# First attention: who adds the relative terms in the two slots of eight that hold two maxima, PE instead of DVE

## What is computed

```python
dist = jnp.clip(jnp.arange(s)[:, None] - jnp.arange(s)[None, :], -MAX_REL, MAX_REL) + MAX_REL   # MAX_REL = 128
rel_pos = rel_emb[dist]
scores = jnp.einsum('bhqd,bhkd->bhqk', q, k)
scores = scores + jnp.einsum('bhqd,qkd->bhqk', q, rel_pos)
scores = scores / np.sqrt(HEAD_DIM).astype(np.float32)
attn = jax.nn.softmax(scores, axis=-1)
local_ctx = jnp.einsum('bhqk,bhkd->bhqd', attn, v)
```

## Time and profile before

| | before |
|---|---|
| median of 3 executions | 3952.41 us (3950.79 to 3961.33) |
| the profiled execution | 3964.92 us, span 3963.1 us |
| PE busy in the span | 3197.3 us (81%) |
| DVE busy | 2230.7 us (56%) |
| ACT busy | 2098.4 us (53%) |
| pair part of groups 0, 1, 2, 3 | 110.34, 111.20, 105.05, 111.19 us |
| all of the first attention's loop, about 127 to 740 us of the span | 613 us |

### The profile page before, as it was taken

One profiled execution on the slowest core, in us unless ns is written; L12 is line 12 of the kernel. 1 busy time (PEld: TensorE's weight loads), 2 busy tenths in 40 slices (PEclk: granted clock), 3 DMA queues, 4 the chain that ended last, 5 costly groups with the idle time before them and its releaser, 6 DMA issues. The chain is left out here.

```text
span 3963.1 us, 72945 instructions
## 1 busy us (share of the span) xinstructions
PE 3197.3 (81%) x24437; PEld 1667.2 (42%) x24437; DVE 2230.7 (56%) x3463; ACT 2098.4 (53%) x3805; POOL 1069.3 (27%) x967
## 2 busy tenths in 40 slices
PE   2788888518920899994699999999999999999997
PEld 1222323113310233331366556556556655655654
DVE  6767677572240777776455555555555555555553
ACT  1466566302210366663366666666666666666664
POOL 0000000003401111110454344345434534533541
PEclk6667587659965799997799999999999999999998
DMA  5221111204445011112211111111111111111111
GB/s 189 81 71 38 54 61 57 75 1 105 101 34 31 23 25 28 26 25 54 100 39 47 39 43 49 30 48 51 33 40 42 50 29 49 53 29 45 42 38 39
DMA packets 191921, 199.77 MB, mean 50 GB/s; under 512 B 113781, under 2 KB 120581, under 8 KB 186794
## 3 DMA queue, kind: packets, MB, share of 16 engines
q1 hardware_dynamic: 154218, 193.05, 17.7%
q10 hardware_dynamic: 37344, 1.97, 1.0%
HBM read 99.64 MB, written 28.97 MB: 32 GB/s over the span
## 5 line engine op out<-in xcount | busy, mean ns | idle before, releaser
L2383 POOL TENSOR_TENSOR tr_t<-tr_t 128x512 f32<-128x512 f32 x384 | 488.9, 1273 | 706.0 <-DVE tr_t L2227 706.0
L2390 POOL TENSOR_TENSOR tr_nq<-tr_t,tr_rn 128x512 f32<-128x512 f32 x384 | 392.6, 1044 | 395.0 <-ACT tr_rn L2123 387.6
L1595 DVE TENSOR_REDUCE attn_mp<-attn_ps 128x1 f32<-128x512 f32 (+3 forms) x660 | 395.2, 656 | 163.9 <-PE attn_ps L1446 86.5
L2088 ACT ACTIVATE tr_pr<-tr_ps 128x768 f32<-128x768 f32 x264 | 213.9, 810 | 375.3 <-PE tr_ps L1910 374.9
L2226 DVE TENSOR_TENSOR tr_t<-tr_ps,tr_tab 128x512 f32<-128x512 f32 x384 | 263.2, 685 | 243.2 <-ACT tr_sq L2097 243.1
L1925 PE MATMUL tr_ps<-tr_w,tr_xs 128*128 128x512 f32 x768 | 372.3, 607 | 29.7 <-DVE tr_xs L2254 26.2
L1557 ACT ACTIVATE attn_pr<-attn_ps 128x768 f32<-128x768 f32 (+2 forms) x352 | 300.9, 870 | 168.1 <-PE attn_ps L1479 165.2
L2236 DVE TENSOR_TENSOR tr_o<-tr_ps,tr_rd 128x384 f32<-128x384 f32 (+1 forms) x264 | 144.0, 545 | 429.3 <-ACT tr_rd L2113 414.0
L678 DVE TENSOR_REDUCE attn_mcol<-attn_ps 128x1 f32<-128x1024 f32 x274 | 332.9, 1220 | 90.8 <-PE attn_ps L523 88.2
L663 ACT ACTIVATE attn_pr<-attn_ps 128x512 f32<-128x512 f32 x512 | 277.8, 599 | 160.6 <-DVE attn_ps L692 146.4
L1910 PE MATMUL tr_ps<-tr_qT,tr_kT 64*128 64x96 f32 (+1 forms) x4224 | 300.9, 282 | 0.0
(11 more groups left out here) (259 smaller groups left out, 5037.2 us busy)
## 6 DMA issues: line engine op xcount, KB each, us to landing
tr_v<-tr_va SPq DMA_DIRECT2D x144, 192.0 KB, 2.6
attn_ka<-scratch_kp SPq DMA_DIRECT2D x72, 294.0 KB
tr_v<-tr_va SPq DMA_DIRECT2D x144, 128.0 KB, 2.4
moe_cb<-scratch_combineT SPq DMA_DIRECT2D x32, 512.0 KB
tr_w<-in_w_half SPq DMA_DIRECT2D x12, 1024.0 KB
tr_v<-tr_va SPq DMA_DIRECT2D x48, 256.0 KB, 2.4
scratch_kp<-proj_parts SPq DMA_DIRECT2D x36, 256.0 KB
attn_km<-scratch_kp SPq DMA_DIRECT2D x72, 98.0 KB
```

The source lines that it names most:

```text
L1595: dve.tensor_reduce(dst, src, AX.X, ALU.max).then_inc(maxed, 1)
L2383: pool.tensor_tensor(t12[:, slot, i, 0, :], t12[:, slot, i, 0, :], t12[:, slot, i, 1, :], ALU.add).then_inc(summed, 1)
L2390: pool.tensor_tensor(nq[:, slot, i, :].rearrange("p (h e) -> p h e", e=DH), t12[:, slot, i, 0, :].rearrange("p (h e) -> p h e", e=DH), rn[ ...
```

## The change

In slots 3 and 7 (`PE_ADDS`) DVE no longer adds. PE does it: behind the bf16 score matmuls of a unit it multiplies `rel` (moving, fp32, 256 or 128 columns) with the fp32 identity (stationary, 128 x 128) and accumulates into the same columns of the bank. ACT's exponential then waits for PE's count (`qk_done`) and no longer for DVE's. In all slots the matmul on the near tiles now comes last of its unit.

```diff
+PE_ADDS = tuple(J for J in range(ST) if TILES_J[J] > 1)
...
 def adds_until(a):
-    return sum(1 for x in range(a + 1) if near_tiles(x // 4, x % 2))
+    return sum(1 for x in range(a + 1) if x // 4 not in PE_ADDS and near_tiles(x // 4, x % 2))
...
-                for v, lo, hi in ((1, 0, near[0]), (0, *near), (2, near[1], S)):
+                for v, lo, hi in ((1, 0, near[0]), (2, near[1], S), (0, *near)):
...
+                if J in PE_ADDS and near_tiles(J, c):
+                    first, count = near_tiles(J, c)
+                    D_ = first - J + 1
+                    mm = pe.matmul(ps[:, unit % 3, (first - 4 * c) * P:(first - 4 * c + count) * P], ident[:],
+                                   rel[:, 2 * p + e, J, D_:D_ + count, :].rearrange("p d i -> p (d i)"), start=False,
+                                   stop=True, skip_group_check=True)
                 mm.then_inc(qk_done, 1)
...
-                            if near_tiles(J, c):
+                            if J not in PE_ADDS and near_tiles(J, c):
                                 act.wait_ge(rel_added, GP * ADDS * g + ADDS * p + adds_until(a) + 1)
...
-                if near is None:
+                if near is None or J in PE_ADDS:
                     return
```

## The result

| | before | after |
|---|---|---|
| median, runs side by side on one chip | 3956.85 us (3950.79 to 3961.33, 4 runs) | 4013.11 us (3992.00 to 4016.53, 4 runs) |
| ratio | 1 | 1.0137 [1.0110, 1.0164] |
| profiled execution, span | 3964.92, 3963.1 us | 4013.86, 4012.1 us |
| PE, DVE, ACT busy | 3197.3, 2230.7, 2098.4 us | 3258.7, 2203.4, 2100.4 us |

The account below looks back on a forecast made before the run. No engine was full; DVE was taken to end slot 3's waits. PE's charges in slots 3 (9.6 + 19.6) and slots 7 (3.5 + 2.9) made 35.6 us, on the median 3952.41 giving 3988 us; range 3956 to 4012 us.

Parts of the forecast that it names:

- Which engine ends the slot: Slot 3: DVE ends the waits before; with DVE off the chain PE is next, 4.7 us instead of 3.67 when fast.
- The price of the identity matmul: Slots 3 and 7: 0.48 us for 256 columns, 0.27 for 128; at the lower clock 0.91 and 0.49.
- the dense price: fp32 passes priced from dense rows with loads hidden: about 0.24 us for 256 columns, 0.136 for 128.
- the forecast's own sum: PE's new work less its idle time: slots 3 9.6 and 19.6, slots 7 3.5 and 2.9, together 35.6 us.
- the upper bound named for it: The fp32 weight load of 0.19 us stands bare before each of the 192 passes: 36 us more.
- DVE's relief is worth nothing: Slots 3 and 7: 37 us of DVE's adds removed, but PE then ends a fast slot 3, so no gain.
- The clock, taken as unchanged: Pair parts: granted clock unchanged on balance, for two opposite reasons; wrong if its mean leaves 0.78 by more than 0.05.
- The new place for a fall: Slot 4 starts behind a full PE and is light itself, so the clock may fall there; no size given.
- The near matmul last: All slots: writing the near matmul last of its unit costs nothing, since the unit is counted only at its end.
- The rest of the program as before: Everything after 780 us, outside the pair parts, stays as before.
- The 0.2 us: Each PE burst ends in some 0.2 us another matmul could use; four bursts in slot 3 free 0.8 us.
- rival 1: Slots 3 and 7: PE has more room, 0.8 us more free in slot 3; sum 18, 3970 us, chance 0.14.

Follow-up runs that it names:

- the kernel with slot 3 alone: The changed kernel with PE's adds in slot 3 only, DVE adding in slot 7 again: 4028.19 us, ratio 1.0158 to before.
- with 64 columns: The changed kernel with its fp32 identity matmuls cut to 64 columns each, the other near columns getting no relative term: ratio 1.0156 to before.
- The kernel without any adds: The changed kernel with the near tiles' relative terms in slots 3 and 7 added by neither DVE nor PE: 3964.10 us, ratio 1.0013.
- the kernel with the order alone: The changed kernel with all adds left to DVE, only the near matmul written last of its unit: 3952.14 us, ratio 0.9999.
- the changed kernel with dummies: The changed kernel plus two dummy bf16 matmuls ahead of the maximum tile in slots 0 and 1 of every pair: 3992.41 us, ratio 1.0102.

## Why the prediction was right

The sign and the place were right; one term was mis-sized.

- **Which engine ends the slot.** Right. Slots 3 and 7 are PE's from end to end; ACT's waits there are put down to PE, 69.5 us. The forecast for slot 3 was 4.7 and 7.9 us, measured 5.30 and 8.94; for slot 7 4.2, measured 4.53. I had called the mechanism wrong below 3.7.
- **The price of the identity matmul.** This is the step that failed: "I take the dense price, since those rows are of the same kind, with their loads hidden." Between these bf16 score matmuls the dense price didn't hold, whether it is the loads or the height. A matmul took 0.63 us of PE for 256 columns and 0.42 for 128 instead of 0.48 and 0.27, and 1.15 and 0.72 instead of 0.91 and 0.49 at the lower clock. Put into the forecast's own sum, which leaves its idle times as they are, these give 9 x 2.10 - 3.90 = 15.0, 7 x 3.74 = 26.2, 12 x 1.26 - 8.01 = 7.1, and 3 x 2.30 + 1.26 - 3.54 = 4.6 us: 53 instead of 35.6. With the slot lengths now measured, at the clock pattern of before, it reads: 9 fast threes x 1.63 = 14.7, 7 slow threes x (8.94 - 5.07) = 27.1, 12 sevens x 0.63 = 7.6, and about 4 for the last sevens (an estimate, since three of them stand at the lower clock in the earlier trace rows and none in the changed profile: a slow seven grew from 5.30 us in the kernel with slot 3 alone to 7.22, by 1.92, of which some 0.6 would fall into idle time as it did with 64 columns). Together about 53 again; measured were 48.5 between the two profiles, whose slots do not stand at the same clocks. The term was short by 13 to 18 us, and the upper bound named for it, 72 us with every load bare, about 20 too high.
- **DVE's relief is worth nothing.** Right, for more than the reason given. I had it that PE takes over. The kernel without any adds shows that the relief would be worth nothing even for free (slot 3 takes 3.67 us with DVE's adds and without any, and the ratio is 1.0013): the chain runs through the second tile and its maximum. The reading that DVE's adds end the waits of slot 3 was wrong in that. DVE's busy time fell by 31 us in the pair parts instead of 37.
- **The clock, taken as unchanged.** Its mean went from 0.79 to 0.80, within the 0.05 named. But that rests on a profile of before that stands 12.5 us above its median; against the 0.83 of the kernel with the order alone it fell, and cost 25 us. The runs show how much room the assumption had: the same slots gave 425 to 438 us between executions, and edits like this one gave clocks from 0.69 to 0.80. The new place for a fall that was named, slot 4 behind a full slot 3, is there in the changed kernel with dummies: in two pairs of group 3 the clock is 0.89 in slot 4 and 0.50 in slots 5 to 7.
- **The near matmul last: nothing.** Right, 0.9999.
- **The rest of the program as before.** Right here, within 3 us; with other edits in the same place the transformer moved by 16, which I had not thought of.
- **The range.** 3956 to 4012 us. The change brought 54 us instead of 36, and by the ratio 4006.6 lies in it, near its upper end; the bare median of these runs, 4013.11, lies 1.1 us above it, and the interval of the ratio, to 4017.2, reaches beyond it. That a sum short by a third still ended inside was in part luck.

The 0.2 us that I had estimated from the earlier trace rows at the end of each burst had spoken for rival 1, with more room on PE than charged. The sums bear out the idle times as charged: a pair got 2 x 0.63 + 2 x 0.42 + 2 x 0.63 = 3.36 us of new matmuls at the upper clock and grew by 26.86 - 24.52 = 2.34, so that 1.02 us went into idle time. The forecast had counted on 3.90 / 9 + 8.01 / 12 = 1.10. Of the further 0.8 us that rival 1 saw in slot 3, nothing was to be had.

## What to carry to other kernels

An engine that is busy in 97% of a slot isn't for that the one that ends it: leave its work out once, and see whether the slot gets shorter, before moving that work to another engine. A small matmul put between others of another type or height is not to be priced from dense rows of its own kind alone: its columns cost the same here, but each matmul brought some 0.15 us more. Read the price as the distance to the next instruction's start, not as the recorded duration, and not as what a slot grew by. And where the clock changes level inside a stage, read each slot at both levels, then count how many stand at each, since a change of 10 us by the clock can hide one of 10 by the work.

## What the runs showed that I had not expected

- A few dummy matmuls in two light slots held the granted clock of the pair parts at 0.94, where the same slots without them had 0.79 and 0.83 in two executions, and made these parts 12 to 24 us shorter (413.9 us against 425.5 and 437.8).
- A stage that no edit touched took 2029.6 or 2045.6 us, by 32 further matmuls that ran once, 1.8 ms earlier.
- An fp32 identity matmul of 64 columns costs more than half of one of 256, 0.37 against 0.63 us, and slot 3 got only 0.29 us shorter by it, in part since PE then waits for an exponential.
